# A masked-attention plus soft-MoE layer: column norms of mu from a transposed copy on ScalarE, their scaling put into the last two blocks, combine's residual queued first, and the last norms beside the logits

## The reference

```python
x = _layernorm(x + attn(x, wq, wk, wv, wo))
x = _layernorm(x + ffn(x, gamma, beta, mu, scale, W1, b1, W2, b2))
# attn: 16 heads, 4 kv heads, rope; mean of a causal and a windowed softmax, then @ wo
# ffn:
x_ln = layernorm(x) * gamma + beta;  x_n = l2norm(x_ln, -1) * scale
mu_n = l2norm(mu, 0)                       # mu is [D=2048, E=16, S=128]
logits = einsum('bnd,des->bnes', x_n, mu_n)
dispatch = softmax(logits, over n);  combine = softmax(logits, over e,s)
slot_in = einsum('bnd,bnes->besd', x_ln, dispatch)
h = gelu(slot_in @ W1 + b1);  slot_out = h @ W2 + b2
out = einsum('bsd,bns->bnd', slot_out, combine)
```

## Time and profile before

| what | us |
|---|---|
| median of 3 runs of the kernel before | 3960.43 |
| its runs | 3956.66, 3960.43, 4450.43 |
| the profiled execution | 3967.46 |
| its span on core 7, the slowest | 3965.9 |
| the other cores' spans | 3926.5 to 3949.0 |
| busy on core 7: PE, DVE, ACT, POOL | 3478.8, 1454.2, 1254.3, 919.2 |

### The profile page before, as it was taken

The page is one execution under the profiler, slowest core; times in us unless marked ns, Lnnn a source line. Parts: engine busy times, 40 slices in busy tenths (PEclk is TensorE's granted clock), DMA queues, the critical chain, the costliest instruction groups (busy, mean ns, idle before and its releaser), DMA issues.

```text
span 3965.9 us, 66989 instructions; the slowest of 8 cores (3926.5 to 3965.9 us)
## 1 busy us (share of the span) xinstructions
PE 3478.8 (88%) x25120; PEld 2130.4 (54%) x25120; DVE 1454.2 (37%) x3138; ACT 1254.3 (32%) x1620; POOL 919.2 (23%) x992
## 2 busy tenths in 40 slices
PE   5767888898897777888988899999979999999998
PEld 3334544655654434546555545677734455777543
DVE  1236655453443465454444422111134322111254
ACT  1123434455551233334456522222101222212111
POOL 3634434343242353343432200000000000000000
PEclk9888989999998888899999999999989999999999
DMA  9965877576444876476411420377685300676743
GB/s 189 210 143 142 156 143 163 133 139 141 112 123 127 169 176 130 128 168 146 122 48 65 165 101 33 111 246 250 238 298 199 141 33 33 218 248 235 281 170 138
DMA packets 131613, 615.77 MB, mean 155 GB/s; under 512 B 15328, under 2 KB 17376, under 8 KB 108768
## 3 DMA queue, kind: packets, MB, share of 16 engines
q1 hardware_dynamic: 106560, 430.06, 31.2%
q0 software_dynamic: 15520, 114.30, 19.4%
q10 hardware_dynamic: 9216, 67.11, 4.2%
HBM read 604.08 MB, written 188.74 MB: 200 GB/s over the span
## 4 chain that ended last, share of the span: by engine, by line
PE 69%; DMA 9%; DVE 6%; issue 5%; POOL 4%; ACT 4%; SPq 1%; another core or an unknown queue 0%; DVEq 0%; ACTq 0%; POOLq 0%
PE ob L1071 11%; PE sc L985 11%; PE pr L454 10%; PE pr L362 9%; PE sc L1265 5%; PE sc L556 5%; PE ob L584 4%; PE sc L1112 3%; PE pr L1265 3%; PE ob L1265 3%; DMA x1sp<-AR 2%; DMA AR<-wqkv_r 2%; DMA AR<-wqkv_c 2%; DMA wqkv_c<-AR 1%; ACT AR L560 1%
## 5 line engine op out<-in xcount | busy, mean ns | idle before, releaser
L362 PE MATMUL pr<-AR 128*128 128x512 bf16 x2560 | 678.1, 402 | 111.6 <-DMA AR<-xT_r 35.7
L560 ACT ACTIVATE AR<-sc 128x1024 bf16<-128x1024 f32 (+2 forms) x640 | 564.0, 895 | 607.8 <-PE sc L556 598.8
L454 PE MATMUL pr<-AR 128*128 128x512 bf16 x2048 | 535.4, 395 | 40.5 <-DMA AR<-wo 15.9
L1071 PE MATMUL ob<-AR 128*128 128x256 bf16 x4096 | 459.6, 273 | 0.0
L985 PE MATMUL sc<-AR 128*128 128x512 bf16 x2048 | 455.0, 380 | 0.0
L444 POOL TENSOR_TENSOR AR<-AR 128x2 f32<-128x2 f32 x64 | 45.0, 703 | 1748.9 <-DVE AR L440 1696.6
L362 PEld LDWEIGHTS pr<-AR 128*128 128x128 bf16 x2560 | 245.4, 102 | 352.8 <-issue 171.1
L1071 PEld LDWEIGHTS ob<-AR 128*128 128x128 bf16 x4096 | 399.4, 98 | 54.5
L556 PE MATMUL sc<-AR 128*128 128x256 bf16 (+1 forms) x2304 | 359.6, 280 | 49.5 <-ACT AR L560 42.8
L584 PE MATMUL ob<-AR 128*128 128x129 bf16 x3840 | 308.9, 225 | 103.7 <-DVE AR L630 54.9
L569 POOL TENSOR_TENSOR AR<-AR 128x256 bf16<-128x256 bf16 x256 | 198.3, 775 | 742.9 <-ACT AR L560 673.0
(11 more groups left out here) (102 smaller groups left out, 3918.4 us busy)
## 6 DMA issues: line engine op xcount, KB each, us to landing
AR<-w_c SPq DMA_DIRECT2D x256, 512.0 KB, 6.6
AR<-wqkv_c SPq DMA_DIRECT2D x168, 512.0 KB, 5.5
w_c<-W_r POOLq DMA_DIRECT2D x32, 2048.0 KB, 20.7
AR<-x SPq DMA_DIRECT2D x32, 1024.0 KB, 6.2
x1sp<-AR ACTq DMA_DIRECT2D x32, 1024.0 KB, 5.7
AR<-b SPq DMA_DIRECT2D x32, 1024.0 KB, 9.5
AR<-x1sp SPq DMA_DIRECT2D x32, 1024.0 KB, 5.2
out<-AR ACTq DMA_DIRECT2D x32, 1024.0 KB, 3.9
```

The lines of the kernel that those rows point to most:

```text
L362: tm = p.pe(lambda e, b=b, c=c, w=w: e.matmul(out=pr[b], lhsT=w[:, c * 128:(c + 1) * 128], rhs=xT[:, c * 512:(c + 1) * 512], start=c == 0, ...
L454: tm = p.pe(lambda e, b=b, h=h, dg=dg, nt=nt, i=i: e.matmul(out=pr[b], lhsT=oT[i % 2][:, nt, h, :], rhs=wo[h][:, dg * 512:(dg + 1) * 512], ...
L560: ta = p.act(lambda e, b=b, eb=eb, lo=lo, hi=hi: e.activation(out=eb[:, lo:hi], in_=sc[b][:, 0:hi - lo], func=AF.Exp), tm, t_E_pe[h % 2])
L1071: tm = p.pe(lambda e, b=b, s=s, c=c, n=n, gp=gp: e.matmul(out=ob[b][:, s * 256:(s + 1) * 256], lhsT=rx[n][:, c * 128:(c + 1) * 128], rhs=E ...
```

## The change

1. **Norms.** A transposed copy of mu, `mu_t`, 64 pieces of 128 slots x 512 values, f32, comes from the host. 64 "m" items (now counts in `MU_AT`, blocks 1, 2, 3, 8, 9, 10, 11) each load one piece by SP's queue and square it on ACT with the sum along the row as a second output. In block 12 DVE adds the four sums of each expert and POOL raises to the power -0.5; SP stores the 128x16 result into `inv_c` in DRAM, transposed element by element, and in blocks 14 and 15 SP reads it back broadcast to all partitions. The ones matrix, L699, L707, L712, L715, L721, L724 and L726 are gone.
2. **Scaling.** At the start of block 14 `scale_all` lays down 16 loads of mu by POOL's DMA (cast to bf16), 16 scalings on DVE, one every 14 ticks, and 16 stores by SP. They use the SBUF of the projection's inputs, which is free by then, and that is where the logits want the slabs: 9 of the 16 stay in place and need no load at the phase's end. Seven of POOL's loads wait for the store that empties their buffer.
3. **Last norms.** `flush()` before the logits is gone: the pending pieces come with 10 ticks after each row tile, and what waits for them (`first_phase_done`) is recorded at tile 4.
4. **Combine's residual.** The tiles use `y2` buffers in the order 2, 0, 1, ...; buffer 2 is loaded after expert 11, and tiles 1 and 2 are queued before the 14 slabs of mu.

```diff
-        def load_mu(e_):
-            t_mu_in[e_] = p.dma("gpsimd", "D_muld", mus, d_mu[e_], t_mu_st[0], t_eb_all[0])
+        def load_mut(j):
+            if j < NE * 4:
+                t_mu_in[j] = p.dma("sync", f"D_mut{j % 3}", mut[j % 3], d_mut[j], t_mu_sq[j % 3],
+                                   t_eb_all[0])
...
+            def square():
+                t_mu_sq[j % 3] = p.act(lambda e: e.activation(
+                    out=mut[j % 3], in_=mut[j % 3], func=AF.Square, accum_out=ssm[:, j:j + 1]),
+                    t_mu_in[j])
...
+            def store():
+                t_inv[0] = p.op("sync", lambda e: e.dma_start(
+                    out=d_inv.rearrange("e s -> s e"), in_=rtmp, allow_slow_non_contiguous=True),
+                    tok[0], sem="D_inv", by=16)
...
+            def load():
+                t_mu_in["s", k] = p.dma("gpsimd", f"D_mus{i}", x, d_mu[e_], t_mu_free[0],
+                                        t_mu_all.get(9 + i) if k >= 7 else None)
...
+            for k in range(NE):
+                if k >= 7:
+                    after(GAP * (k - 7) + 30, steps[k][0])
+                after(GAP * k + 20 + (40 if k >= 8 else 0), steps[k][1])
+                after(GAP * k + 25 + (40 if k >= 8 else 0), steps[k][2])
...
-        MU_AT = {1: [0, 1, 2], 2: [3, 4, 5], 3: [6, 7, 8], 8: [9], 9: [10, 11, 12], 10: [13, 14, 15]}
+        MU_AT = {1: 11, 2: 9, 3: 11, 8: 5, 9: 11, 10: 9, 11: 8}
...
         for j in range(9):
-            load_mu_slab(j, t_proj_end)
+            sl_tok[j] = t_mu_use[7 + j]
...
-        flush()
...
                 tl = logits(n, 1)
                 if n:
                     turn_e(n - 1, 1)
+                for _ in range(10):
+                    tick()
+                if n == 4 and el == 0:
+                    t_misc = [first_phase_done()]
...
+                if b == 11:
+                    t_y2[2] = t_si_free[2]
+                    load_y2(0)
...
+            t_y2[0] = t_y2[1] = [t_so[14], t_so[15], t_ffn]
+            load_y2(1)
+            load_y2(2)
             if el == 0:
                 for j in range(14):
                     load_mu_slab(j, t_ffn)
```

More of the change, by code:

```diff
@@ L876, in build_program @@
             c_proj = 4.2 * n_it * (2.0 if i == 15 else 1.0)
-            if i in MU_AT and MU_AT[i][0] in (0, 9):
-                load_mu(MU_AT[i][0])
+            if i in (min(MU_AT), 8):
+                for j in range(3):
+                    load_mut((0 if i < 8 else MU_HALF) + j)
+            if i == max(MU_AT) + 1:
+                mu_norms()
+            if i == 14:
+                scale_all()
             pre = list(pre_at[i])
@@ L1083, in disp, with load_y2 @@
                 return tm
+            t_yx2 = {}
+            t_y2 = [None] * 3
+            row = [(n + 2) % 3 for n in range(NCH - 1)] + [0]
+            def load_y2(n):
+                i = row[n]
+                t_yx2[n] = p.dma("sync", f"D_y{i}", y2[i],
+                                 d_x1[el, n * 128:(n + 1) * 128, :], t_x1[el, n], t_y2[i])
             t_b2 = {}
```

163 lines of the change are left out of this document (87 added, 76 removed).

## The result

The changed kernel takes 3911.51 us in the median (runs of 3906.64, 3907.38, 3915.63 and 4111.53). Its ratio to the kernel before is 0.9877, with a 95% interval of 0.9845 to 0.9909: a real gain, smaller than 2%. By the medians 48.9 us are gained, where 57.4 were forecast. The profiled execution took 3915.63 us; its span is 3913.9 us on core 5, the slowest.

The account below looks back on a forecast made before the run. PE bounds the second phase apart from two holes, PE's waits at a falling clock the first. 3967.5 - 24.6 (first phase) - 9.6 (last norms) - 23.2 (combine) = 3910.1, less 7.0 above the median: 3903 us; range 3867 to 3940.

Parts of the forecast that it names:

- Parts 3 and 4: Start of logits and start of combine: PE's holes and the slower matmuls after them go, -9.6 and -23.2 us.
- Rival (c): Combine's hole stays because the residuals of tiles 1 and 2 still come too late: 3926 us, chance 0.08.
- Part 1, norms and squares: First phase: 16 norms gone at 4.85 us each, 77.6 gained; 64 squares on ACT at a quarter us, 16 lost.
- the twins say what it is worth with its stalls: Blocks 3 and 11 differ by three norms: 16.8 us on core 7, 12.3 on core 4, so 5.6 and 4.1 a norm.
- The store of the norms: Block 12: the transposed store of 2048 separate 4-byte elements costs nothing; ends 0 and some 10 us.
- slab loads late in block 12: A listed sign, in block 12, that the prediction is wrong; no size given.
- Part 2, scaling: Blocks 14 and 15: sixteen scalings on DVE at 2.0 us each, 32 us lost; ends 0 and 55.
- somewhat more than half will meet: Blocks 14 and 15: share of scalings meeting a mask pair, at a price between 0 and 3.44 us each.
- POOL's waits: Blocks 14 and 15: seven mu loads wait for stores with masks queued behind, 5 us lost; ends 0 and 69.
- Rival (d): Block 14: POOL loads waiting for stores hold the masks and PE, making the kernel slower: 3990 us, chance 0.03.
- Rival (a): First phase: the clock pays too, 24 us in four blocks, and norms another 12: 3867 us, chance 0.18.
- rival (b): First phase nets nothing, squares at 0.6 us and scalings at 3.44 eating the gain: 3928 us, chance 0.18.

Follow-up runs that it names:

- b_nomu: Kernel before, norms left out and mu cast DRAM to DRAM on GpSimd's queue without waits; the six norm blocks took 823.1 us, against 865.0 before.
- a_nosq: Changed kernel with each square taken of one column instead of 512; blocks 0 to 15 took 2218.9 us against 2218.3.
- b_plan: Kernel before with the planner's count of the projections cleared of norm items; blocks 0 to 15 took 2212.3 us, against 2234 before.
- a_plan: Changed kernel with no norm items in the planner's cost of projections; block 11 fell from 140.8 to 133.4 us, blocks 0 to 15 took 2208 against 2218.
- a_invrow: Changed kernel with inverse norms turned by VectorE and stored as rows; ratio to before 0.9849, block 12 fell from 140.1 to 126.3 us.
- a_pre8: Changed kernel, planner's count without norm items, block 8's three weight casts moved to blocks 4, 7 and later; blocks 0 to 15 took 2191 us.
- a_split: Changed kernel with every scaling cut into four pieces of 512 columns; ratio to before 0.9873, blocks 14 and 15 fell from 241.9 to 234.6 us.
- a_noscale: Changed kernel with row stores, norm-free count, spaced mu loads, block 8's casts in block 15, scaling pieces of one column; blocks 14 and 15 231.4 us, against 237.7 with full pieces.

## Why the prediction was right and wrong

The time was near, but steps of the sum failed: the transposed store was put at nothing and cost 14 us, the planner's count was not priced at all, block 8 lost where a gain was forecast, and norms and scalings were priced too high. They are taken one by one.

**Parts 3 and 4: right.** Forecast 9.6 and 23.2 us, measured 10.7 and 22.4. PE runs there without a break, and a stall with one releaser and nothing behind it is worth its own length plus what the clock loses. Rival (c) is out.

**Part 1, norms and squares: right in the sum by luck, wrong in both terms.** For the five blocks with 15 norms I had -72.8 us, and +12.8 for their 51 squares, so -60.0; measured -61.7. But a norm was worth 4.0 us, not 4.85 (`b_nomu`), and a square 0, not 0.25 (`a_nosq`). The step that failed is that "the twins say what it is worth with its stalls", that is, that the whole difference of blocks 3 and 11 (16.8 and 12.3 us on the two cores, 14.4 in the mean of eight) is the price of three norms: leaving their work out gives 8.9, their loads to SBUF, stores and waits 2.9 more, and 2.6 are left. The planner's count alone, which I had suspected, does not give them (`b_plan`). Where the norms' work, their traffic in POOL's queue and the count are all gone, the twins are level (133.8 and 133.4 in `a_plan`), so it is no lasting difference between the two windows; how the causes share it stays open. And the sum agrees because errors cancel: the count cost 13 us of these five blocks in the changed kernel (647.9, and 635.0 in `a_plan`) and 24 in the kernel before (709.6, and 686.0 in `b_plan`).

**The store of the norms: put at nothing, a step that failed.** "I put it at nothing, as four slabs of the ring are ahead of it; ends 0 and some 10 us": it cost 14 us (`a_invrow`). The four slabs did not cover it: on four cores the store took 60 to 75 us and held the issuing engine, and on all of them the casts and the slab loads beside it took longer, the slab loads 11.9 us instead of 5.4 in the median on core 7. My upper end came from waits for contiguous stores, which say nothing of 2048 elements. Of the prediction's signs of being wrong, "slab loads late in block 12" came.

**The planner's count: not seen.** The diff let `n_it` count 5 to 11 norm items a block instead of 1 to 3, and 8 in block 11, which had none. I had block 11 at +2 us for its squares; it took +7.8, and `a_plan` gives 7.4 of it back. The clock's fall with it in block 11 is small, 0.94 against 0.95, and PE is busy 1.2 us longer, so the rest of the 7 us is idle PE, in the second half of the block. The count's whole price is larger: its removal gives 31 us in blocks 3, 10, 11 and 12 (in 12 together with the store) and costs 11 in block 8.

**Block 8: not seen.** Forecast -3.6 us, measured +7.2: a slab load beside two or three casts. That the casts make it is shown (`a_pre8`: 133 us); that the change made it worse by shifting the casts against the slabs is an inference from the distances of the casts and the holes that go with them (4.6 us before, 18.0 after); no run moved the casts alone within the block.

**Part 2, scaling: too dear.** 37 us forecast for blocks 14 and 15 (32 for the scalings and 5 for POOL's waits), 19.4 measured, and of these some 3.5 belong to the first scaling's wait for its reads, which the prediction did not have. That a scaling costs by locking DVE and the masks in one stretch was right in kind (`a_split`); that "somewhat more than half will meet" a mask pair at up to 3.44 us was not: 7 of 16 met a mask, four masks were stretched, and PE's waits for masks in the two blocks grew from 0.5 to 3.4 us on core 5. By `a_split` (7.3) and `a_noscale` (6.4) the 16 scalings cost at most some 14 us, an estimate of 0.9 each where I took 2.0. POOL's waits for stores were 15.1 us in all, against 19.2. Rival (d) is out.

**Taken together:** errors of +14.2 (block 12, store), +5.8 (block 11, count), +10.8 (block 8), -17.6 (scaling), -1.7 (norms and squares) and some -3 in the blocks not touched leave the first phase 8.5 us above the forecast, and 1.4 come from the second. The net was near the forecast by luck, because a large error went the other way. Rival (a), a clock that pays too, did not come: block 1 has 0.86 on core 5 now instead of 0.81 on core 7, but the norms' blocks gained 61.7 us in all, about what I had without (a). Nor did rival (b): the first phase did net 16 us, and of its two costs the squares took nothing and the scalings at most some 14 us instead of 55.

## What to carry to other kernels

A DMA of single elements is to be priced by its landing time, by the DMAs of all queues beside it and by the engine that issues behind it, not by its bytes; turn the values on chip and store rows. Look at more than one core before you take a wait for the mechanism: here half of them lost 11 us without it, the others 17. When a change adds entries to a list, look for every place that counts the list: here a planner's cost. And before two blocks are taken as twins, take out the suspected work alone once; a part of their difference may be its transfers, or something else altogether.

## What the runs showed of the hardware that I had not expected

A DMA issue that otherwise takes 0.3 to 0.4 us held the issuing engine far longer behind an element-wise store: 26.77 us on SP and 13.73 us on ACT (core 5), which computed nothing meanwhile, and this on four of the eight cores. The 8 KB store landed from SP's queue after 60.4 to 74.9 us on those cores and after 19.7 to 23.1 us on the others, from ACT's queue after 55.4 to 59.0 and 14.8 to 17.9, while casts ran beside it (DMA share 0.88 in block 12 of core 5). Where nothing was held, the 2 MB casts of the block took 29.1 us instead of 17.4. A slab load of 512 KB, 5.2 us to landing in the median of the page, took 34.4 us in block 8 beside the 2 MB casts. And a 128x2048 product on DVE took 2285 ns in one piece but 4 x 765 = 3060 ns in four, and the four cost the kernel less; a mask of 128x256 on POOL took 2.53 us beside the one piece, 0.67 us alone.
